# A two-layer mixture-of-experts kernel: GpSimd splits the first weights ahead of most of its small loads, and the first router's matmuls go behind the first two expert units

## The reference

```
x = x + L0_ffn(L0_cond(x, cond_64))
x = x + L1_ffn(L1_cond(x, mask, null_kv=cond_64))
```

```
logits = (x @ wt.T + repeat(g @ wg.T)) / 2
scores = softmax(logits);  top-2 of 8, renormalised
y = sum over the chosen experts of w * (leaky(x @ w_gate[e]) * (x @ w_up[e])) @ w_down[e]
y = y + (leaky(x @ sw_gate) * (x @ sw_up)) @ sw_down
```

## Time and profile before

| | |
|---|---|
| median of 3 runs | 379.27 us (378.29 to 380.31) |
| span of the profiled execution, first to last instruction | 375.1 us |
| what lies around the span (median less span) | 4.2 us |
| busy: PE, DVE, ACT, POOL | 271.3, 257.9, 165.0, 160.1 us |
| mean granted TensorE clock | 0.896 |

### The profile page before, as it was taken

How to read it: one execution, slowest core, us unless ns; L and a number is a source line. 1 busy time by engine, 2 the same in 40 slices (tenths; PEclk the granted TensorE clock), 3 DMA queues, 4 the chain that set the end, 5 groups by cost and what they waited for, 6 DMA issues and landing times.

```text
span 375.1 us, 5005 instructions
## 1 busy us (share of the span) xinstructions
PE 271.3 (72%) x1777; PEld 208.1 (55%) x1777; DVE 257.9 (69%) x441; ACT 165.0 (44%) x261; POOL 160.1 (43%) x177
## 2 busy tenths in 40 slices
PE   4575729879409985756658778765665999999984
PEld 3553415646309873644537555553554788887763
DVE  2249835694266879897556657652466999999994
ACT  2223501563200022544232243423979399999850
POOL 8985431000056310000054655652403857698852
PEclk9979959999958996698669999999889699999998
DMA  8940180000996400000000000008006600000001
GB/s 188 257 75 0 47 183 0 0 1 17 193 222 111 175 4 0 2 0 0 2 2 3 2 2 2 0 3 224 0 2 204 248 0 2 2 0 2 0 0 56
DMA packets 25751, 20.87 MB, mean 56 GB/s; under 512 B 10304, under 2 KB 20341, under 8 KB 25728
## 3 DMA queue, kind: packets, MB, share of 16 engines
q1 hardware_dynamic: 24864, 20.10, 21.2%
q0 software_dynamic: 864, 0.46, 1.3%
HBM read 19.84 MB, written 0.72 MB: 55 GB/s over the span
## 4 chain that ended last, share of the span: by engine, by line
PE 33%; DVE 28%; POOL 14%; DMA 10%; ACT 7%; issue 6%; SPq 1%; POOLq 0%; DVEq 0%
PE ps L779 9%; PE ps L780 8%; PE ps L781 8%; DMA arena<-comb_f 5%; PE ps L847 3%; POOL arena L533 2%; DMA arena<-comb_c 2%; POOL rstd L514 2%; POOL arena L524 2%; DVE n L1351 2%; DVE arena L1282 2%; DVE g_lo L1484 2%; DVE arena L1358 2%; DVE arena L1202 2%; DVE ssum L1411 1%
## 5 line engine op out<-in xcount | busy, mean ns | idle before, releaser
L779 PE MATMUL ps<-act_hi,w_hi 128*128 128x512 f32 x120 | 51.6, 430 | 26.0 <-ACT att_bias L763 7.5
L1484 DVE TENSOR_TENSOR g_lo<-att_bias,g_hi 128x1024 fp32r<-128x1024 f32 x32 | 59.0, 1878 | 1.3 <-ACT g_hi L769 0.7
L780 PE MATMUL ps<-act_lo,w_hi 128*128 128x512 f32 x120 | 49.0, 409 | 0.0
L781 PE MATMUL ps<-act_hi,w_lo 128*128 128x512 f32 x120 | 48.7, 406 | 0.0
L763 ACT ACTIVATE att_bias<-ps,vec 128x512 f32<-128x512 f32 x64 | 41.9, 686 | 10.2 <-PE ps L781 10.1
L779 PEld LDWEIGHTS ps<-act_hi,w_hi 128*128 128x128 f32 x120 | 23.9, 199 | 38.1 <-issue 29.8
L567 POOL TENSOR_TENSOR act_lo<-f_down,act_hi 128x512 fp32r<-128x512 f32 x16 | 28.0, 1750 | 28.9 <-ACT act_hi L726 28.8
L524 POOL TENSOR_TENSOR arena<-arena,smax 128x528 f32<-128x528 f32 x8 | 8.6, 1073 | 56.1 <-DVE smax L1404 56.1
L498 POOL TENSOR_TENSOR arena<-arena 128x512 f32<-128x512 f32 x6 | 10.2, 1730 | 52.1 <-DMA arena<-comb_f 52.1
L893 PE MATMUL ps<-f_down,arena 128*128 128x128 f32 x144 | 18.4, 293 | 14.1 <-DVE arena L1282 14.1
L590 POOL TENSOR_TENSOR k_diag<-k_diag 128x512 f32<-128x512 f32 x14 | 23.3, 1663 | 12.2 <-DVE k_diag L1518 12.2
(11 more groups left out here) (274 smaller groups left out, 667.9 us busy)
## 6 DMA issues: line engine op xcount, KB each, us to landing
arena<-comb_f SPq DMA_DIRECT2D x4, 1024.0 KB, 15.5
arena<-gate_m SPq DMA_DIRECT2D x8, 512.0 KB, 7.7
arena<-comb_c SPq DMA_DIRECT2D x4, 512.0 KB, 9.0
w_stage<-in_L_ffn_W SPq DMA_DIRECT2D x1, 2048.0 KB, 11.8
w_stage<-in_L_ffn_W SPq DMA_DIRECT2D x8, 256.0 KB, 4.4
x_tok<-in_x SPq DMA_DIRECT2D x2, 256.0 KB, 3.1
w_stage<-in_L_ffn_w_gate SPq DMA_DIRECT2D x1, 512.0 KB, 5.1
w_stage<-in_L_ffn_w_up SPq DMA_DIRECT2D x1, 512.0 KB, 5.5
```

Of the source, the lines that this page charges most:

```text
L779: pe.matmul(dst, wh, xh, start=first, stop=False)
L780: pe.matmul(dst, wh, xl, start=False, stop=False)
L781: return pe.matmul(dst, wl, xh, start=False, stop=last)
L1484: dve.tensor_tensor(g_lo[:, k % 2, b, :], gelu[:, k % 2, b, :], g_hi[:, k % 2, b, :].bitcast(f32), ALU.subtract).then_inc(v_glo, 1)
```

## The change

Four edits, all in the first 45 us.

1. GpSimd makes its tables, then runs `split(0)` to `split(4)`, then issues 17 of the small loads (position network 8, norms 5, routers 4), then `split(5)`, then the other 10 (attention), then clears the tables and goes on with `split(6)`.
2. PE computes the logits of the first four token tiles behind unit 0 and of the other four behind unit 1.
3. ScalarE rounds half 1 of the tokens behind `chunk(4)` and computes the exponential behind the gate copy of unit 2.
4. VectorE turns half 0 ahead of the router's small copies and half 1 behind them, and takes units 0 and 1 ahead of the softmax; each later piece of the router stands one unit further on.

```diff
@@ gpsimd
-            for t, name, rows in ((0, "L1_ffn_ln_g", 8), ...):
-                pool.dma_start(vec_rows[t:t + rows, :], a[name]).then_inc(ld["vec"], 16)
...
+            small_tables()
             for n in range(CH_N):
                 split(n)
+                if n == C_PAIRS:
+                    position_inputs()
+                    norm_inputs()
+                    router_inputs()
                 if n == C_BLK:
+                    attention_inputs()
 
                     pool.memset(k_diag[:, :, :, :], 0.0).then_inc(ready, 1)
@@ scalar
             chunk(0)
-            for s in range(HALVES):
-                copy_hi(s)
+            copy_hi(0)
             for n in range(1, CH_F):
                 chunk(n)
-            act.wait_ge(v_z, 1)
-            act.activation(r_s[:, :, 0:C_EXP], r_z[:, :, 0:C_EXP], ACT.Exp).then_inc(act_exp, 1)
-
+            copy_hi(1)
...
             for u in range(2 * C_BLK):
                 gate_copy(u)
+                if u == 2:
+                    act.wait_ge(v_z, 1)
+                    act.activation(r_s[:, :, 0:C_EXP], r_z[:, :, 0:C_EXP], ACT.Exp).then_inc(act_exp, 1)
                 if CH_F + u < CH_N:
                     chunk(CH_F + u)
@@ tensor
-            pe.wait_ge(v_small, 3)
-
-            for t in range(TILES):
+
+            def first_logits(t):
                 pe.wait_ge(v_T, t // HT + 1)
...
-            mm.then_inc(pe_log, 1)
...
                 up_unit(u, C0, C_BLK, s, b, s + 1, s + 1, b + 1)
+                if u == 0:
+                    pe.wait_ge(v_small, 3)
+                if u < 2:
+                    for t in range(u * HT, (u + 1) * HT):
+                        mm = first_logits(t)
+                if u == 1:
+                    mm.then_inc(pe_log, 1)
@@ vector
+            dve.wait_ge(pe_xT, 1)
+            turned(0, bank(4), 0)
             dve.wait_ge(pe_small, 1)
...
-            for s in range(HALVES):
-                dve.wait_ge(pe_xT, s + 1)
-                turned(s, bank(4 + s), 0)
+            dve.wait_ge(pe_xT, 2)
+            turned(1, bank(5), 0)
...
+            c_unit(0)
+            c_unit(1)
             dve.wait_ge(pe_log, 1)
...
-            c_unit(0)
+            c_unit(2)
             dve.wait_ge(act_exp, 1)
...
-            c_unit(1)
             dve.wait_ge(ready, 6)
             rank8(e8)
-            c_unit(2)
+            c_unit(3)
             link(dve.scalar_tensor_tensor(z, r_rank[:, :, 0:8], 1.5, e8, ALU.is_lt, ALU.mult))
...
-            c_unit(3)
```

More of the change, by code:

```diff
@@ L436, in _ @@
[L436 to L452, removed]
@@ L453, in _ @@
-            pool.dma_start(router_b[:, :], a["L1_ffn_router_b"].partition_broadcast(P)).then_inc(ld["gk"], 16)
-            for n, name in enumerate(("q_scale", "k_scale")):
-                pool.dma_start(qk_scale[:, n, :], a["L1_cond_" + name].partition_broadcast(P))\
-                    .then_inc(ld["att"], 16)
-            pool.dma_start(null_b[:, :], a["L1_cond_null_attn_bias"].partition_broadcast(P)).then_inc(ld["att"], 16)
-            pool.dma_start(g_out[:, :], a["L1_cond_g_out"].partition_broadcast(P)).then_inc(ld["att"], 16)
@@ L459, in _, with small_tables @@
[L459 to L465, removed]
+            def small_tables():
+                for t, n in ((ahead8, 8), (ahead4, 4)):
+                    link(pool.memset(t[:, :, :], 0.0))
+                    pool.affine_select(out=t[:, :, :], in_=t[:, :, :], compare_op=ALU.is_gt, fill=TINY, base=0,
+                                       pattern=[[1, n], [-1, n]], channel_multiplier=0).then_inc(ready, 1)
+                pool.iota(pos_i[:, :], pattern=[[0, 1]], base=LEN - 1, channel_multiplier=-1).then_inc(ready, 1)
+                pool.iota(iota_i[:, :], pattern=[[1, F_EXP]], base=0, channel_multiplier=0).then_inc(ready, 1)
@@ new lines, in position_inputs @@
+            def position_inputs():
+                for n, name in enumerate(("w0", "b0", "g0", "b1", "g1")):
+                    src = a["L1_cond_" + name]
+                    src = src[0, :] if name == "w0" else src
+                    pool.dma_start(rp_rows[:, n, :], src.partition_broadcast(POSN)).then_inc(ld["rp"], 16)
+                pool.dma_start(rp_w1[:, :], a["L1_cond_w1"]).then_inc(ld["rp"], 16)
+                pool.dma_start(rp_w2[:, :], a["L1_cond_w2"]).then_inc(ld["rp"], 16)
+                pool.dma_start(rp_b2[:, :], a["L1_cond_b2"].unsqueeze(1)).then_inc(ld["rp"], 16)
@@ new lines, in router_inputs, with norm_inputs @@
+            def router_inputs():
+                pool.dma_start(gk[:, 0:F_EXP], a["L0_ffn_gate_kernel"]).then_inc(ld["gk"], 16)
+                pool.dma_start(f_bias[:, :], a["L0_ffn_gate_bias"].partition_broadcast(P)).then_inc(ld["gk"], 16)
+                pool.dma_start(router_w[:, 0:M_EXP], a["L1_ffn_router_W"]).then_inc(ld["gk"], 16)
+                pool.dma_start(router_b[:, :], a["L1_ffn_router_b"].partition_broadcast(P)).then_inc(ld["gk"], 16)
+            def norm_inputs():
+                for t, name, rows in ((0, "L1_ffn_ln_g", 8), (8, "L1_ffn_ln_b", 8), (48, "L1_ffn_b2", 8)):
+                    pool.dma_start(vec_rows[t:t + rows, :], a[name]).then_inc(ld["vec"], 16)
+                pool.dma_start(vec_rows[V_B1:V_B2, :], a["L1_ffn_b1"].rearrange("e (b p) -> (e b) p", p=P))\
+                    .then_inc(ld["vec"], 16)
+                pool.dma_start(vec_rows[V_GN:V_ROWS, :], a["L1_cond_g_norm"].unsqueeze(0)).then_inc(ld["vec"], 16)
@@ new lines, in attention_inputs @@
+            def attention_inputs():
+                for n, name in enumerate(("q_scale", "k_scale")):
+                    pool.dma_start(qk_scale[:, n, :], a["L1_cond_" + name].partition_broadcast(P))\
+                        .then_inc(ld["att"], 16)
+                pool.dma_start(null_b[:, :], a["L1_cond_null_attn_bias"].partition_broadcast(P))\
+                    .then_inc(ld["att"], 16)
+                pool.dma_start(g_out[:, :], a["L1_cond_g_out"].partition_broadcast(P)).then_inc(ld["att"], 16)
+                for s in range(BPT):
+                    pool.dma_start(mask_u8[s * LEN:(s + 1) * LEN, :, :],
+                                   a["mask_BxS_bf1"].rearrange("(t s) j -> s t j", s=BPT)[s].partition_broadcast(LEN))\
+                        .then_inc(ld["att"], 16)
+                for h in range(2):
+                    pool.dma_start(nv_col[h * DH:(h + 1) * DH, :], a["cond_64"][1, :].unsqueeze(1))\
+                        .then_inc(ld["att"], 16)
@@ L802, in _ @@
                 pe.matmul(o, act_T[:, t * P:(t + 1) * P], wt_T[:, :], start=True, stop=False)
-                mm = pe.matmul(o, g_tok_T[:, t * P:(t + 1) * P], wg_T[:, :], start=False, stop=True)
-            mm.then_inc(pe_log, 1)
+                return pe.matmul(o, g_tok_T[:, t * P:(t + 1) * P], wg_T[:, :], start=False, stop=True)
             def up_unit(u, base, blocks, s, b, hi_need, lo_need, ch):
```

## The result

The changed kernel takes 381.58 us (379.0 to 383.83), before in the same comparison 378.47 us: a ratio of 1.0074, 95% interval 1.0052 to 1.0097. It is slower by 0.7%, where 372.9 was forecast, in a range of 371.4 to 376.2. The profiled execution's span is 378.4 us (375.1 before), at a mean granted clock of 0.889. Medians here are over all executions; the ratios to the kernel before leave out the few that fell into the chip's slow state.

A forecast was written before the change was run, and what follows sets the result against it. GpSimd's small loads bound the first 19 us, then VectorE's list up to comb_T's copy. Unit 2 6.7 us earlier and VectorE's terms put that copy at 34.5 against 40.91: 379.3 - 6.4 = 372.9, range 371.4 to 376.2.

The forecast's parts named there:

- Part 1: GpSimd's list: five splits done by about 12.3, 17 loads by 21.7, other 10 by 27.9, clears by 32.
- Parts 2 and 3: First units on PE: subtraction stretched +0.3 beside a split, unit 0 at 10.4, unit 2 at 18.5, 6.7 us earlier.
- Part 4: VectorE's path from unit 2 to the copy of comb_T: 34.5 against 40.91, 6.4 us earlier.
- the weights ... 1.15: Part 4's term for the routing weights on VectorE: 1.58 before, taken as 1.15 without splits beside it.
- rival (a): PE's clock falls after a 2.6 us pause; unit 6 takes 2.9 instead of 1.66: 1.3 us, 374.2; chance 0.32.
- Rival (b): GpSimd's load issues block VectorE's instructions with two SBUF operands: 13 at 0.54 make 7.0, time 379.9; chance 0.03.
- Rival (c): VectorE lengthens GpSimd's load issues by 0.54 each; norms' last lands at 30.7, 2.5 us lost, 375.4; chance 0.05.

The follow-up runs named there:

- e9: Kernel before with only the changed kernel's GpSimd list, GpSimd also waiting for the end of each clear and each later split: 372.90 us, ratio 0.9824.
- e4_probe: Changed kernel with three more small one-input additions on VectorE between units 0 and 1, beside GpSimd's issue of loads: 381.36 us in one run.
- e11_one_gap: Changed kernel with one added wait: GpSimd waits for the end of its first clear before issuing the second: 374.93 us, ratio 0.9878.
- e6_hold_gaps: Changed kernel with GpSimd waiting behind each clear and later split, all held back until VectorE's first position step is done: 372.83 us, ratio 0.9842.
- e3: Changed kernel with GpSimd's five clears moved ahead of its first split: 374.57 us, ratio 0.9888.
- e7: Kernel before with only GpSimd's list of the changed kernel, old orders on PE, ScalarE and VectorE: 370.83 us, ratio 0.9762.

## Why the prediction was wrong

- **Part 1** held: splits from 8.66 to 12.6 (12.3 forecast), loads to 21.7, the other ten to 27.9, clears to 32.0. No load was late.
- **Parts 2 and 3** held: VectorE's subtraction beside a split took 0.73 instead of the 0.99 taken, unit 0 began at 10.04, unit 2 at 18.55 (18.5 forecast); PE's rows went from 0.63 to 0.39 at 14.77, 4.7 us behind the start of unit 0, between the 3.8 and 5.9 that the prediction had read from two places of before.
- **Part 4 failed in one term**, "the weights ... 1.15". Up to it the sum was right: unit 3 was done at 26.5 (26.4). The term holds the addition of line 1174 at its duration alone (0.17 in before), and it took 7.79: 7.6 us. The rest of the 8.8 us between 34.5 and 43.26 is unit 6 at the low clock, 2.93 from its first matmul to its gate copy instead of 1.66. That is rival (a)'s price and not its cause: the pause of 2.6 that it feared was survived (2.61 ahead of unit 5), and the clock fell in the pause of 9.49 that the wait made. The length of a pause alone does not tell: in e9 one of 2.15 was followed by a matmul of 0.77.
- **What I had seen and mispriced.** I took the stretching of VectorE's instructions beside splits (0.26 and 0.54 in the earlier trace rows) for the bound of any meeting of the two engines, one instruction's length. In those rows no more than one split stood ready behind the running one. The row of 0.95 looks like the opposite, three splits back to back behind the clears. But line 1119 at 29.25 was let in ahead of the second split, and the third could not be ready yet, since ScalarE was still rounding its chunk. Two rows of before, the second split by itself and that rounding:

```profile
29.61 1.17 POOL L471 TENSOR_TENSOR w_lo<-w_stage,w_hi 128x256 fp32r<-128x256 f32 x1
29.47 0.41 ACT L606 ACTIVATE w_hi<-w_stage 128x256 fp32r<-128x256 f32 x1
```

For the changed kernel's five splits behind the clears all chunks were rounded by 29.22, before the first of them began. I also counted the clears as cover that "ends at 32", and asked only who waits for them, not what they stand beside. In before they stood beside unit 1 and `rank8`, of which nothing was caught (0.69 and 0.68 beside clears); the change moved them 3 us later and line 1174 5 us earlier, so that the unbroken run met line 1174.
- **Rival (b)** named the right engines and the wrong GpSimd work. In the changed kernel line 1139 (four times) and the two first steps of `rank8`, all with two inputs from SBUF, ran beside the issue of loads between 13.6 and 25.8 in 0.69 each, and e4_probe shows the additions passing there in 0.19 each. That the kernel came out slower, as (b) says, is no merit of (b): one instruction made the loss, not thirteen.
- **Rival (c)** did not happen, and its price was too high. By the prediction's own sum unit 6 could not start before 30.2, so rows landing at 30.7 would have cost under 1 us, not 2.5.
- The Trainium skill's "SBUF — State Buffer", section "Who interferes with whom", which I used for 0.4 us, tells which instructions can meet: copies, casts and operations with a scalar against any GpSimd work, where they run in a mode that uses the port pair shared with GpSimd, and instructions with two SBUF inputs against GpSimd's reads. The runs agree with that division: the addition, the casts and the scaling were held beside clears and splits, line 1142 beside splits (4.68) and not beside clears (0.69). It says that the loser waits for the whole instruction of the other; here it waited for six to ten of them in a row, and e11_one_gap ends that with one wait.
- By e6_hold_gaps, in which nothing was held on the way to comb_T, the other terms add up to the forecast: 372.83 against 372.9, comb_T copied by 33.9 against 34.5. It is part luck: comb_T came 0.6 us early, and from its copy to the products it took 11.0 us instead of the 10.6 of before, so that these start at 44.65 (44.8 forecast).

## What to carry to other kernels

When a change moves GpSimd's work, lay each unbroken run of it beside VectorE's list and look for copies, casts and operations with a scalar from SBUF to SBUF, and beside GpSimd's reads for instructions with two SBUF inputs. Behind long clears the price was the rest of the run, not one instruction. A wait of GpSimd on its own last result, or its long clears put where VectorE idles, cut it to one GpSimd instruction, at most 1.83 us in the five runs that tried it. A duration far from that of its like in the timeline can be a wait, though the lists of waits are silent. Try the parts of a change apart: here the half that was worth having (0.976) was hidden behind the one that cost (1.014) and behind what only the two together set off.

## What the runs showed of the hardware that I had not expected

- A small VectorE instruction (0.17 to 0.34 us alone) was held for 6.97 to 8.12 us by back-to-back GpSimd instructions, in five kernels; each time it was let in when about one instruction of the run was left. That fits a rule by which VectorE gets its turn once GpSimd's queue holds no more than one further instruction, and so does the row of 0.95 in before; but in e3 the cast was let in after the first split although the next three chunks had long been rounded, so it is not the whole rule. What in the queue decides the moment was not settled; that a single wait of GpSimd on its own result opens the way was.
- With unbroken clears to follow, the hold begins already during the loads issued ahead of them, up to 1.3 us before the first clear (the addition at 26.36 to 26.97 in three kernels, the cast at 27.02 in a fourth), while with a wait behind the first clear, or with no clear there, the addition passed beside the same loads in 0.17 to 0.90.
- Splits held an instruction that reads SBUF twice (4.68 us) as well as those that read it once; clears were seen to hold only the latter. Copies out of PSUM passed beside a clear in 0.21 and 0.27 (e7).
